# Attention scores turned in three products instead of four: key low parts moved into the other head's rows, query high parts twinned

## The reference

```
q = heads(x @ Wq); k = heads(text @ Wk); v = heads(text @ Wv)
probs = softmax(q @ k.T / 4);  text_out = probs @ v
layer 0: text = the 77 tokens; image tokens: none left over (the slice behind 77 is empty)
layer 1: text = the first 73 tokens, 4 image tokens:
   qsem = l2norm(probs @ text);  sem = qsem @ l2norm(ip).T
   probs_ip = softmax(q @ k_ip.T / 4 + 0.5 * sem) * spatial_mask
   out = text_out + probs_ip @ v_ip
x = x + out @ Wo + bias        (after each layer)
```

## Time and profile before

| | |
|---|---|
| median of 3 runs | 2455.07 us (2453.14 to 2455.76) |
| profiled execution, first to last instruction | 2447.7 us |
| PE busy | 2259.4 us (92%) |
| DVE busy | 1702.0 us (70%) |
| ACT busy | 1728.4 us (71%) |
| POOL busy | 1592.2 us (65%) |

### The profile page before, as it was taken

How to read it: one execution, slowest core, us unless ns; L and a number is a source line. 1 busy time by engine, 2 the same in 40 slices (tenths; PEclk the granted TensorE clock), 3 DMA queues, 4 the chain that set the end, 5 groups by cost and what they waited for, 6 DMA issues and landing times.

```text
span 2447.7 us, 90636 instructions
## 1 busy us (share of the span) xinstructions
PE 2259.4 (92%) x35896; PEld 1464.0 (60%) x35896; DVE 1702.0 (70%) x2860; ACT 1728.4 (71%) x2604; POOL 1592.2 (65%) x1056
## 2 busy tenths in 40 slices
PE   8999958999999999999999999999999999999984
PEld 6777735655566665666556555666566655555642
DVE  5543425777777777777777777777777777777763
ACT  4332327778878777787787787877877787787861
POOL 4121135777777777777777776777777777777762
PEclk9999969999999999999999999999999999999996
DMA  9968622444444444444344444444444444444421
GB/s 275 281 209 235 194 89 70 117 115 117 118 114 114 118 115 116 118 115 117 111 118 119 115 114 114 113 118 115 115 118 118 114 113 115 114 119 116 119 80 56
DMA packets 338318, 310.92 MB, mean 127 GB/s; under 512 B 180224, under 2 KB 281856, under 8 KB 337920
## 3 DMA queue, kind: packets, MB, share of 16 engines
q1 hardware_dynamic: 337920, 305.36, 44.7%
HBM read 164.66 MB, written 105.98 MB: 111 GB/s over the span
## 4 chain that ended last, share of the span: by engine, by line
PE 46%; DVE 23%; ACT 7%; issue 5%; DMA 3%; SPq 2%; DVEq 0%; POOL 0%; ACTq 0%; POOLq 0%
PE psum L1065 12%; PE psum L966 10%; PE psum L1049 8%; PE psum L1028 7%; DVE q_low L1220 4%; ACT q_high L1136 4%; DVE mneg L1213 3%; PE psum L969 3%; ACT ef L1154 3%; DVE e L1235 3%; DVE sq L1254 2%; DVE outt L1313 2%; PE psum L1032 2%; PE psum L991 2%; DVE x1b L1313 1%
## 5 line engine op out<-in xcount | busy, mean ns | idle before, releaser
L1381 POOL TENSOR_TENSOR e<-ef,eh 73x1024 f32<-73x1024 f32 x320 | 681.1, 2129 | 300.4 <-ACT eh L1169 257.0
L1154 ACT ACTIVATE ef<-psum 73x1024 f32<-73x1024 f32 (+1 forms) x640 | 628.0, 1011 | 90.9 <-PE psum L1032 87.4
L1235 DVE TENSOR_TENSOR e<-psum,e 73x1024 f32<-73x1024 f32 x320 | 386.7, 1209 | 135.6 <-PE psum L1065 135.3
L1213 DVE TENSOR_REDUCE mneg<-psum 128x8 f16<-128x616 f32 (+3 forms) x512 | 446.9, 923 | 34.9 <-PE psum L991 34.1
L1065 PE MATMUL psum<-eh,gram 128*73 128x512 f16 x1280 | 340.9, 390 | 45.2 <-ACT ef L1154 16.0
L1049 PE MATMUL psum<-ef,values 128*32 128x256 f32 x5120 | 351.4, 389 | 7.7 <-DVE pip L1295 5.9
L1028 PE MATMUL psum<-q_high,keys 32*73 32x256 f16 (+2 forms) x6144 | 324.7, 258 | 34.0 <-DVE mneg L1213 21.6
L1169 ACT ACTIVATE eh<-ef 73x1024 f16<-73x1024 f32 x320 | 337.0, 1053 | 16.2 <-ACT ef L1154 0.4
L1220 DVE SCALAR_TENSOR_TENSOR q_low<-psum,q_high 128x640 f16<-128x640 f32 x128 | 105.5, 824 | 262.3 <-ACT q_high L1136 262.3
L1028 PEld LDWEIGHTS psum<-q_high,keys 32*73 32x73 f16 (+1 forms) x6144 | 186.9, 110 | 144.5 <-issue 68.7
L1162 ACT ACTIVATE ust<-psum 128x512 f32<-128x512 f32 x384 | 223.4, 594 | 67.1 <-PE psum L1049 60.5
(11 more groups left out here) (180 smaller groups left out, 4530.3 us busy)
## 6 DMA issues: line engine op xcount, KB each, us to landing
rb<-r_dram SPq DMA_DIRECT2D x128, 384.0 KB, 4.1
keys<-k_dram SPq DMA_DIRECT2D x128, 231.0 KB, 3.6
values<-v_dram SPq DMA_DIRECT2D x128, 192.5 KB
ust<-ust SPq DMA_DIRECT2D x512, 48.0 KB, 2.5
v_dram<-vst SPq DMA_DIRECT2D x64, 320.0 KB
out<-outt SPq DMA_DIRECT2D x64, 320.0 KB, 2.2
k_dram<-kst SPq DMA_DIRECT2D x32, 616.0 KB, 4.8
x<-in_x SPq DMA_DIRECT2D x32, 384.0 KB, 3.7
```

The source lines that it names most:

```text
L1154: act.activation(ef[l][0:m, unit_heads(n), :].rearrange("t h s -> t (h s)"), src, ACT.Exp, scale=SM).then_inc(s_exp[l], 1)
L1213: dve.tensor_reduce(dst, o, AX_X, ALU.max, negate=True).then_inc(s_max[l], 1)
L1235: dve.tensor_tensor(rest, banks(l, f"u{k}", 2)[0:m, :, :], rest, ALU.mult).then_inc(s_wr, 1)
L1381: pool.tensor_tensor(e2[0:m, k, :, :], ef[1][0:m, unit_heads(k), :], eh[0:m, unit_heads(k), :], ALU.subtract).then_inc(s_e2, 1)
```

## The change

In the first part DVE moves the low key parts by 16 rows within each group of 32, into the rows that hold zeros in the high tile (`stream_shuffle` in place, on pairs of float16 seen as int32, `move_lows`), and then adds the high part on top (`join_parts`), so that the tile of low parts holds both parts: the head's high part in its own rows and its low part in the other head's. This is done once a pair of column blocks or a tail is complete, behind the first DVE instruction of the following product; the key stores wait for it.

In the second part DVE makes two copies of the query's high part (`twins`, steps `tw0` and `tw1` behind `ql`): in copy `e` the 16 rows of head `e` stand in both halves of each 32 rows. The turned scores take the high key with the low query, then the tile of both parts with the twin, then the maxima. The rough scores and the image-token scores are as before.

```diff
+TWIN = [[e * D + i % D for i in range(SLOT)] for e in (0, 1)]
+OTHER = [(i + D) % SLOT for i in range(SLOT)]
 ORDER "dve":
-  ... 1ql/2 1s0/2 1s1/2 1s2/2 1s3/2 1w3/3 0d/1 1w4/3 0ql/0 1p/4 0s0/0 ...
+  ... 1ql/2 1tw0/2 1tw1/2 1s0/2 1s1/2 1s2/2 1s3/2 1w3/3 0d/1 1w4/3 0ql/0 0tw0/0 0tw1/0 1p/4 0s0/0 ...
 # SP, first part
                 def results_of(kind, l, half):
+                    if kind in ("k", "kt"):
+                        b.reached(sp, s_kboth, 2 * 6, slot * 6 + half * 3 + (l if kind == "k" else 2) + 1)
+                        return
 # DVE, first part
+            def move_lows(u):
+                kind, l, _, half = KV_USES[u]
+                lows = keys_part(kind, l, half, 1).bitcast(I32)
+                dve.stream_shuffle(lows, lows, OTHER).then_inc(s_klow, 1)
+            def join_parts(b, slot, u):
+                kind, l, _, half = KV_USES[u]
+                b.reached(dve, s_klow, 2 * 6, slot * 6 + half * 3 + (l if kind == "k" else 2) + 1)
+                highs, lows = (keys_part(kind, l, half, low) for low in (0, 1))
+                dve.tensor_tensor(lows, lows, highs, ALU.add).then_inc(s_kboth, 1)
...
+                    before = u - 1 if u and KV_USES[u - 1][0:3:2] in (("k", 1), ("kt", 0)) else None
+                    if before is not None:
+                        wait_taken(dve, b, slot, before)
                     if kind in ("k", "kt"):
                         for e in (0, 1):
...
+                            if e == 0 and before is not None:
+                                move_lows(before)
...
                     ins.then_inc(s_taken[False], 1)
+                    if before is not None:
+                        join_parts(b, slot, before)
 # PE, second part
                 if c == 0:
                     b.reached(pe, s_ql[l], 1, 1)
+                    b.reached(pe, s_tw[l], 2, 2)
...
-                    for low, q in ((0, qh[l]), (0, ql[l]), (1, qh[l])):
+                    for both_parts, q in ((0, ql[l]), (1, twin[l][:, e, :].bitcast(F16))):
                         for rows, o in tiles:
-                            pe.matmul(o, keys(l, low, c)[rows, e, 0:n], q[rows, cols], start=(low == 0 and q is qh[l]),
+                            pe.matmul(o, keys(l, both_parts, c)[rows, e, 0:n], q[rows, cols], start=(both_parts == 0),
                                       stop=False)
 # DVE, second part
+        twin = [sb(f"twins{l}", [P, 2, PW // 2], I32) for l in both]
+            def twins(l, b, e):
+                b.reached(dve, f_t[l], CW, 0)
+                b.reached(dve, s_qh[l], 1, 1)
+                dve.stream_shuffle(twin[l][:, e, :], qh[l][:].bitcast(I32), TWIN[e]).then_inc(s_tw[l], 1)
```

More of the change, by code:

```diff
@@ L133 @@
     "dve": """
-        1y10/4 1y11/4 0o/2 1y12/4 1y13/4 1y14/4 1w2/3 1y15/4 1y16/4 1y17/4 1y18/4 1y19/4 1ql/2 1s0/2 1s1/2
-        1s2/2 1s3/2 1w3/3 0d/1 1w4/3 0ql/0 1p/4 0s0/0 0s1/0 0s2/0 1d/3 0s3/0 1w0/2 1w1/2 1y0/3 1y1/3 1y2/3
+        1y10/4 1y11/4 0o/2 1y12/4 1y13/4 1y14/4 1w2/3 1y15/4 1y16/4 1y17/4 1y18/4 1y19/4 1ql/2 1tw0/2 1tw1/2 1s0/2 1s1/2
+        1s2/2 1s3/2 1w3/3 0d/1 1w4/3 0ql/0 0tw0/0 0tw1/0 1p/4 0s0/0 0s1/0 0s2/0 1d/3 0s3/0 1w0/2 1w1/2 1y0/3 1y1/3 1y2/3
         1y3/3 1o/4 1y4/3 1y5/3 1y6/3 1y7/3 1y8/3 1y9/3""",
@@ L264, in keys_and_values @@
         cl = sb("cl", [P, 2, EC, CT], F16)
-        kst = [sb(f"kst{l}", [P, 2, HB, 2, 2, 2, T], F16) for l in both]
-        ktail = sb("ktail", [P, 2, HB, 2, 2, T], F16)
+        kst = [sb(f"kst{l}", [P, 2, HB, 2, 4 * T], F16) for l in both]
+        ktail = sb("ktail", [P, 2, HB, 2, 2 * T], F16)
         kist = sb("kist", [P, 2, CW, CB * IP], F16)
@@ L284, in keys_and_values @@
         s_khigh = sem("key_highs")
+        s_klow, s_kboth = sem("key_lows_moved"), sem("keys_with_both_parts")
         s_taken = {True: sem("kv_taken_by_act"), False: sem("kv_taken_by_dve")}
@@ L355, in store @@
                         results_of("k", l, half)
-                        keys = kst[l][:, half, :, :, :, :, :].rearrange("p b h c e t -> p b (h c e t)")
+                        keys = kst[l][:, half, :, :, :].rearrange("p b h n -> p b (h n)")
                         sp.dma_start(dst[l][:, :, 0:8 * T], keys).then_inc(s_kstored[half], 16)
@@ L360, in store @@
                         for copy in (0, 1):
-                            tail = ktail[l * HALF:(l + 1) * HALF, half, :, :, :, :].rearrange("p b h e t -> p b (h e t)")
+                            tail = ktail[l * HALF:(l + 1) * HALF, half, :, :, :].rearrange("p b h n -> p b (h n)")
                             sp.dma_start(dst[l][copy * HALF:(copy + 1) * HALF, :, 8 * T:], tail)\
@@ L507, in by_head, with keys_part @@
             return ap.rearrange("p (h d) -> p h d", d=D)
+        def keys_part(kind, l, half, low):
+            if kind == "k":
+                return kst[l][:, half, :, low, :]
+            return ktail[:, half, :, low, :]
         def half_keys(kind, l, c, half, low, e):
             if kind == "k":
-                return kst[l][:, half, :, low, c, e, :]
-            return ktail[:, half, :, low, e, :]
+                return kst[l][:, half, :, low, (2 * c + e) * T:(2 * c + e + 1) * T]
+            return ktail[:, half, :, low, e * T:(e + 1) * T]
         def wait_stored(eng, b, slot, kind, half, l):
@@ L772, in attention @@
         s_xh, s_xl, s_rs = [early.s_xh, sem("x_high1")], [early.s_xl, sem("x_low1")], pair("residual")
-        s_qh, s_ql = pair("q_high"), pair("q_low")
+        s_qh, s_ql, s_tw = pair("q_high"), pair("q_low"), pair("twins")
         s_max, s_mt, s_exp = pair("maxima"), pair("maxima_turned"), pair("exponentials")
@@ L792, in wait_free, with keys @@
             turn_banks.wait(eng, freed, b, l, *uses)
-        def keys(l, low, c):
-            lead = low * 4 * T + c * 2 * T if c < 2 else 8 * T + low * 2 * T
+        def keys(l, both_parts, c):
+            lead = both_parts * 4 * T + c * 2 * T if c < 2 else 8 * T + both_parts * 2 * T
             return ke[l][:, lead:lead + 2 * T].rearrange("p (e t) -> p e t", e=2)
@@ L1314, in output @@
                                          ALU.add).then_inc(s_xo[l], 1)
-            program("dve", {"s": maxima, "ql": query_rests, "d": inverses, "w": weighted, "y": ip_softmax,
+            program("dve", {"s": maxima, "ql": query_rests, "tw": twins, "d": inverses, "w": weighted, "y": ip_softmax,
                             "p": attended_ip, "o": output})
```

## The result

The changed kernel takes 2459.57 us at the median of 17 runs (2455.83 to 2472.56), the kernel before 2453.14 us in 17 runs beside it (2446.0 to 2460.93). The ratio is 1.0037, 95% interval 1.0024 to 1.0049: slower by 9 us (6 to 12; the two medians alone differ by 6.4), where 29 to 31 us were forecast. The sign was right and the size too large by a factor of three.

A forecast was written before the change was run, and what follows sets the result against it. PE was taken to bound the kernel, though not alone, since it waits mostly for DVE. Terms of +0.42 us a batch gave +27 us over 64 batches, with +2 us in the first part: 2484 us, range 2447 to 2525.

The forecast's parts named there:

- layer 0's twins ahead of `1t1`: DVE's twins stand uncovered in the chain to the maxima that PE waits for: 0.90 us more a batch.
- layer 1's twins ahead of `1m`: DVE's idle time and slack cover 0.64 of the twins' 0.90 us; the rest delays PE by 0.26 us a batch.
- `0t1`: Layer 0's removed matmuls in block 1, behind the output wait and ahead of `1q`: 0.20 us saved a batch.
- `1t0`: Layer 1's removed matmuls in block 0, ahead of `0q` with no wait of their own: 0.22 us saved a batch.
- `1t1`, `1t2`: Layer 1's removed matmuls in blocks 1 and 2, the former ahead of exponentials: 0.22 and 0.10 us saved a batch.
- `0t2`: Layer 0's removed matmuls in block 2, between `1q` and the wait for `q_low`: 0.11 us removed, nothing gained.
- `0t0` and the wait of `1u2`: Layer 0's removed matmuls in block 0, ahead of PE's wait for DVE's reading of `0o`: 0.22 us removed, nothing gained.
- the first part: DVE's added moves and additions mostly covered; only the first chunk's backlog meets no slack: 2 us more (0 to 8).
- Rival 1: Twins cheaper, the shuffle moving two elements a cycle, about 0.5 us a pair: 2441 us; chance 0.13.
- rival 2: Twins dearer through table loading or a slower stream: 2509 us at 1.1 us a pair, 2535 at 1.3; chance 0.14.
- Rival 3: Layer 0's twins held until POOL is done, costing 1.05 us more a batch: 2551 us; chance 0.05.
- Rival 4: The whole cut arrives, twins hidden, PE losing up to 1.10 us a batch: 2385 us; chance 0.04.

The follow-up runs named there:

- e7: The kernel before with the twins made at the places of the change, PE waiting for them without use: 2489.44 us, ratio 1.0172.
- e4: The kernel before with DVE's reading of layer 0's output two steps earlier: 2438.66 us, ratio 0.9942.
- e8: The kernel before with `sq` written to PSUM instead of SBUF, its two later products scaling the input again: 2434.84 us, ratio 0.9941.
- e3: The changed kernel with layer 0's twins and layer 1's second twin moved behind their layer's last maxima: 2442.11 us, ratio 0.996.
- e6: The changed kernel without the second part's shuffles, twins cleared once at the start, PE's work kept: 2436.97 us, ratio 0.9949.
- e5: The changed kernel with the twins moved as in e3 and layer 0's output read early as in e4: 2424.33 us, ratio 0.9892.
- e10: e5 with POOL's `vb` moved behind layer 0's `xl`: 2419.66 us, ratio 0.9858.

## Why the prediction was right in sign and wrong in size

The term by term comparison, in us a batch:

| step | forecast | measured |
|---|---|---|
| layer 0's twins ahead of `1t1` | +0.90 | +0.73 (e7: +0.74) |
| layer 1's twins ahead of `1m` | +0.26 | +0.25 (e7: +0.25) |
| `0t1` | -0.20 | -0.15 |
| `1t0` | -0.22 | -0.22 |
| `1t1`, `1t2` | -0.32 | -0.23 |
| `0t2` | 0 | 0 |
| `0t0` and the wait of `1u2` | 0 | -0.27 |
| sum | +0.42 | +0.09 |

**The step that failed** is the one for `0t0`: "The wait runs from the end of `0o`; nothing is gained." With it falls what was said of layer 0's twins, "so no other term gives it back". The wait of 0.41 us had DVE's `x1b` as its releaser, and I took it that DVE reads `0o` as soon as it is done. In truth DVE was late by 0.27 us (e4, e8), busy with small steps behind `sq`, and `sq` was held for POOL. I had the earlier trace rows in hand and used it only to ask whether the twins could be held, not what the held instruction already delayed. In a kernel whose engines go round together a second chain that ends at about the same time is a floor: it eats savings (e3, e6: 0q to 1u2 at 18.24 whatever PE saves) and it forgives delays of the same size (e7: -0.27). The twins' +0.73 and the savings of `1t1` and `1t2` lie in that one stretch, and what shows of them is 18.47 - 18.24 = +0.23 us. The sum should have been made for each chain, and the larger taken.

**A size was off** for layer 0's twins: 0.90 for 0.76. The distance of like instructions was the row to go by, and behind another instruction even 0.41 of the 0.52 us counts. With the waits in between, the term is 0.17 x 64 = 11 us too large; the floor is 0.27 x 64 = 17 us. Against them stand 0.14 x 64 = 9 us that `0t1`, `1t1` and `1t2` saved less than I counted, and together these make 19 of the 20 us of the error.

**What the removed products saved.** `0t1` gave 0.15 us, for I took all of the 0.30 us between the end of `xl` and `1q` as room. After the change `1q` starts 0.15 us behind `xl` (median; the shortest of all batches is 0.14), so only half of it was room. `1t1` gave 0.21 us up to `1u0`. `1t2` is 0.12 us shorter itself, but `1u1` to `1o` grew by 0.09, which leaves 0.03; why is not shown.

**Right:** the removed groups (0.22 us for `1t0`), the price of a shuffle by its elements, that `0t2` gives nothing, the 0.1 us more of waits for `q_low`, and that the first part costs next to nothing (+2 forecast, 1.6 measured; DVE from 42 to 68 of 100 us).

**Right by luck:** the +0.26 us of layer 1. I had 0.90 us for the pair and 0.64 us of cover. The pair takes 0.82 us there (1428.50 to 1429.32), and the 0.15 us ahead of `1m` were no cover, since `1m` still starts 0.14 us behind the maxima. What covers is DVE's idle time alone, and the two errors cancel. Luck is also in the first part. Its additions were priced at 1.49 us for 1232 elements; 26 of the 32 took 786 to 799 ns, 0.64 ns an element and not 1.09. The other six began while POOL's `cl` ran, took 1.8 to 2.6 us and ended 0.66 us behind it. I had written that the additions lie under cover. The first one does not: PE's new wait of 0.98 us stands behind it. How much of the wait goes if the addition is not held was not tested.

**The rivals.** Rival 1 (cheap shuffle) and rival 2 (dear one) fall with the 521 ns and the 13 ns. Rival 3 was right about the mechanism and wrong about the victim: no twin is held, but `sq` is, and so are six additions. Rival 4 falls with the 45.1 us of new waits. Of what I said would show in the profile, the wait of `1t1` at 1.25 us was wrong in form (0.6 us of it stands one step earlier, at the second rough scores), and so was the new wait of L1005: layer 1's delay is met at `1s1`. The waits for `x1a` and `x1b` did not grow, (13.8 + 12.2)/56 = 0.46 us against 0.45: another sign of the floor.

**What the change is worth.** With DVE's twins where they are free and with the chain to `x1` shortened, the saved product shows: e5 against e4, which has the same early reading, 31.11 against 31.40 us a batch and ratios 0.9892 against 0.9942. That is about 0.3 us of the 1.10 us by which the removed groups shorten PE's work. Where the rest would stop next is shown only for `0q` (e10).

## What to carry to other kernels

Before counting a delay or a saving on the bounding engine, find for each wait between two points of the loop whether its releaser was itself late, and follow that chain back: a second chain of nearly the same length turns savings into waits and swallows delays. New work of DVE belongs where DVE waits for something that comes later than its end, not behind the value that it is made from; the same four shuffles delay PE by 0.98 us a batch where the change put them (0.71 us net in e7, 0.32 net in the changed kernel against e6), and by nothing in their new places. A short instruction whose duration varies tenfold was here one that another engine held, and its place in the chain was worth a look before any other edit: sending its output to PSUM brought 15 us (e8), more than this whole change cost.

## What the runs showed of the hardware

- A held DVE instruction: 96x64 float32 from SBUF to SBUF took 180 to 2167 ns over all runs that have it so. In the kernel before 58 of 64 took longer than 240 ns, and each of these ended 0.05 us behind a POOL instruction that had been running. With the output in PSUM it took 213 to 225 ns in 64 instances.
- A float16 addition with two inputs in SBUF, 1232 elements, took 786 to 799 ns in 26 instances and 1.8 to 2.6 us in the six that began while a POOL instruction ran; these ended 0.66 us behind it.
- Shuffles from SBUF to SBUF are not held. Of the 256 twins of the changed kernel 122 ran wholly while a POOL instruction ran, in 505 to 545 ns; the 128 beside which POOL did nothing took 503 to 537. All of them (min/median/max ns):

```profile
L1258 DVE STREAM_SHUFFLE twins<-q_high x256: 503/515/545, 327.4 to 2390.4; 128x320 int32<-128x320 int32 x128
```

- The table of rows for a shuffle is loaded in 13 ns and delays nothing that shows: two shuffles with different tables start 0.41 us apart.
